# A four-layer graph network on one core: pair records on 16-byte places, edge weights from 64-row products, and a reordered second addition

## Chip, cores, metric

The kernel runs on one core of a Trainium2 chip. The metric is the device time of one execution in microseconds, median of the runs. Engines: PE is TensorE's matmul and PEld its weight load, DVE is VectorE, ACT is ScalarE, POOL is GpSimd, SP is SyncE. A name with a q (DVEq) is the engine's sequencer: waits, register steps, register loads and the issue of transfers.

## Reference

A graph of 3125 nodes (160 features: 64 scalars and 32 vectors of 3) and 100,000 edges passes through four message-passing layers. Each layer normalizes the nodes, maps them linearly to a table, gathers a table row for every edge, multiplies it (in layers 0, 1 and 3) by weights that a small network of the edge's attributes gives, adds the result over the edges of each target node, multiplies the sums by weights and updates the nodes. Layer 0, cut to its core:

```
w = relu(edge_feature @ W_fc1) @ W_fc2                  # 64 -> 64 -> 224 per edge
xs, xv = s[dst], v[dst]
out0a = w0 * xs                                         # and four more products of w with xs, xv and the edge's direction
agg = segment_sum(concatenate([out0a, ...]), src, N) / 32
node += gate(agg @ W_out + skip)
```

Layer 1 has 10 attributes and 100 hidden units, layer 3 has 8 and 64; layer 2 has no such network: it adds the gathered rows, scaled by the edge's 4 direction values.

## The kernel before, in words

**Tiles.** Edges are sorted by target. A tile is 128 edges (one per partition) whose targets lie in one bin of 32 nodes. There are 880 tiles, in 110 groups (GROUPS) of GT = 8; a group is PAIRS = 4 pairs. The first part of the program ranks the edges by bins, scatters and copies the edge rows into tile order in DRAM (POOL's scatters L752, SP's and ACT's copies L522 to L526) and makes small tables: for each tile its bin, its first node, its column and the half group in which that column has arrived (tiles, L1300 to L1343; written to DRAM by SP from L625, and read back after layer 0 into `guide`, one record of RECORD = 18 words per group: 8 bins, 8 places in the ring, 2 counts).

**Edge stage.** Per layer (LAYERS, n = 0 to 3) an edge stage of 110 groups runs on all engines, each with its own loop over pairs of groups (pipeline), tied by semaphores:
- SP loads the group's edge rows (edge_rows, L609).
- POOL gathers table rows for 128 edges with one indirect transfer: in layer 0 once per tile (L881, 880 of them), in layers 1 to 3 once per column of 128 sorted edges (L920, 782 of them) into a ring of 16 columns. It waits for landings three gathers behind (landed_column, L896) and, per half ring, until the columns' tiles have been used (`free`, loaded by L906, 4 words).
- PE transposes the edge rows (turn, L1854/L1857), forms the hidden units of the next group at u = 2 (hidden, L1864 for layer 0, L1867 for 1, L1871 for 3), per pair the edge weights (weights, L1891) and, two pairs later, the sums over edges (sums, L1915 and L1917; L1911 in layer 2). PE is in order: at step u it does weights(i), sums(i - 2), then turn or hidden.
- ACT turns the hidden units into SBUF (L1067) and builds the selection matrices, 24 or 32 activations a group (L1084).
- DVE, for each pair i, first adds the sums of pair i - 3 to the accumulators (flush, L1495, two additions, where each waits until the one before has ended, since both may hit one bin), then multiplies weights and gathered rows (products, L1509 and L1512 for one tile in layers 1 and 3, L1525 and L1529 in layer 0). At u = 2 it makes the one-hot matrix of the next group (select, L1476, L1486). At the head of each group it loads registers: 8 bins in layer 0 (L1538), the 18-word record in layers 1 and 3, its first 8 words in layer 2 (L1542); in layer 2 PE loads 10 words of it (L1924).

A helper (L99) computes values to wait for from loop registers. The weights of both tiles of a pair go into one PSUM bank (4 or 5), 224 columns apart. The weight matrices of layers 0 and 3 stand twice, in rows 0 to 63 and 64 to 127 with zeros in the other half, and the product runs over all 128 rows; in layers 1 and 3 the hidden products do the same with four or two copies. A float32 product is two records of PE and two of PEld in the trace.

Between edge stages the sums are turned and multiplied by the layer's weights and the nodes updated (node steps).

## Time and profile before

| | us |
|---|---|
| median of 3 runs (lowest, highest) | 8134.93 (8115.99, 8168.47) |
| span of the profiled execution | 5998.2 |
| PE busy in the span | 4489.1 |
| POOL busy | 4014.9 |
| DVE busy | 3441.9 |
| ACT busy | 3414.1 |

The profile gives the profiled execution's span, from its first to its last instruction. Of that execution no other time is given; the median of the runs is 2136.7 us longer, and that part lies outside of what the profile shows. In timeline rows the columns are start, duration, engine, line, operation, names, shapes, count and in brackets the idle time before; in a row of one line they are the count, the durations in ns (lowest/median/highest) and the first and last start in us.

### The profile page before, as it was taken

The page shows a single profiled execution, that of the slowest core. Times are in us where ns is not written, and L with a number is a line of the kernel's source. Part 1 is how long each engine was busy: PE and PEld are TensorE (multiplying, and loading weights), DVE is VectorE, ACT ScalarE, POOL GpSimd, SP SyncE. Part 2 cuts the span into 40 slices and gives each one's busy share as a digit, 9 for nine tenths or more (in the row PEclk, how much of TensorE's full clock was granted, in tenths as well). Part 3 has the DMA queues.
Part 4 walks back from the last instruction along what each step waited for, and adds up shares of the span by engine and source line. Part 5 has one row for each costly group of instructions (what it writes and reads, how often), then busy time and mean ns, then how long its engine had stood idle before and what let it go on. Part 6 is the DMA issues. An engine that isn't in the chain of part 4 may idle for free.

```text
span 5998.2 us, 122036 instructions
## 1 busy us (share of the span) xinstructions
PE 4489.1 (75%) x24426; PEld 3923.9 (65%) x24427; DVE 3441.9 (57%) x11481; ACT 3414.1 (57%) x14717; POOL 4014.9 (67%) x4467
## 2 busy tenths in 40 slices
PE   7793121599999998788888886555555888888888
PEld 5552110588888888788888885444444877777777
DVE  8894000577777776566666664333333666666666
ACT  0000000366555554677777776677778677777775
POOL 6777777677777764676666646777777376666654
PEclk8896555799999999899999996555555899999999
DMA  8533333344444441222222212333333122222221
GB/s 307 181 80 74 80 79 82 77 88 88 87 88 88 88 87 36 71 73 70 68 68 65 64 48 69 77 78 77 78 79 79 44 74 70 68 67 64 64 62 41
DMA packets 643946, 484.25 MB, mean 81 GB/s; under 512 B 437482, under 2 KB 551593, under 8 KB 643707
## 3 DMA queue, kind: packets, MB, share of 16 engines
q0 software_dynamic: 181776, 292.84, 19.4%
q1 hardware_dynamic: 379563, 149.21, 10.3%
q10 hardware_dynamic: 82496, 40.92, 2.3%
q8 instruction: 45, 0.74, 0.1%
q14 instruction: 66, 0.54, 0.0%
HBM read 400.40 MB, written 96.88 MB: 83 GB/s over the span
## 4 chain that ended last, share of the span: by engine, by line
issue 28%; PE 22%; DVE 11%; DMA 9%; DVEq 6%; POOL 4%; ACT 1%; POOLq 1%; SPq 0%; ACTq 0%
DMA gath<-table,rows 6%; DVE acc L1495 5%; PE bank L1915 4%; PE bank L1891 4%; PE bank L1917 4%; PE bank L1867 3%; DVEq L1542 3%; PE bank L1911 2%; DMA gath<-table,small 2%; PE bank L1971 2%; DVE work L1512 2%; DVE work L1509 2%; POOL gath L920 2%; POOL gath L881 2%; DVE work L1529 1%
## 5 line engine op out<-in xcount | busy, mean ns | idle before, releaser
L920 POOL DMA_INDIRECT gath<-table,small x2346 | 2226.1, 949 | 1069.8 <-issue 611.7
L1084 ACT ACTIVATE sel<-acc,rows 128x32 f32<-128x32 f32 x10560 | 2292.6, 310 | 302.3 <-DVE acc L1486 247.6
L1495 DVE TENSOR_TENSOR acc<-acc,bank 128x160 f32 (+1 forms) x3520 | 1207.4, 343 | 1476.3 <-issue 583.1
L1915 PE MATMUL bank<-work,sel 128*128 128x160 f32 (+1 forms) x5280 | 1353.2, 339 | 342.4 <-DVE acc L1495 342.0
L1915 PEld LDWEIGHTS bank<-work,sel 128*128 128x128 f32 x5280 | 914.5, 196 | 420.0 <-DVE acc L1495 396.4
L1917 PE MATMUL bank<-work,sel 128*128 128x160 f32 x5280 | 1181.1, 306 | 0.0
L1891 PE MATMUL bank<-w,work 128*128 128x224 f32 (+2 forms) x5280 | 1153.8, 342 | 17.6 <-DVE work L1529 8.9
L881 POOL DMA_INDIRECT gath<-table,rows x880 | 832.0, 945 | 348.2 <-issue 196.2
L1891 PEld LDWEIGHTS bank<-w,work 128*128 128x128 f32 (+1 forms) x5280 | 915.7, 195 | 89.7 <-issue 52.1
L1917 PEld LDWEIGHTS bank<-work,sel 128*128 128x128 f32 x5280 | 937.8, 196 | 44.7
L752 POOL DMA_INDIRECT rows_a<-acc x782 | 754.6, 965 | 280.3 <-issue 237.5
L1911 PE MATMUL bank<-gath,sel 128*128 x1760 | 554.5, 491 | 450.6 <-POOLq L896 277.3
L1911 PEld LDWEIGHTS bank<-gath,sel 128*128 128x128 f32 x1760 | 454.3, 325 | 550.8 <-issue 550.8
L1067 ACT ACTIVATE work<-bank 100x512 f32<-100x512 f32 (+1 forms) x440 | 250.6, 596 | 786.3 <-PE bank L1871 283.8
L1084 ACT ACTIVATE sel<-sel,rows 128x32 f32<-128x32 f32 x2640 | 582.2, 308 | 124.6 <-DVE sel L1486 97.1
L1512 DVE TENSOR_TENSOR work<-bank,gath 128x192 f32<-128x192 f32 x1760 | 610.9, 347 | 0.0
L1509 DVE TENSOR_TENSOR work<-bank,gath 128x128 f32<-128x128 f32 x1760 | 499.8, 284 | 76.2 <-PE bank L1891 33.0
L1529 DVE TENSOR_TENSOR work<-bank,gath 128x288 f32<-128x288 f32 x880 | 357.1, 447 | 0.0
L997 ACT ACTIVATE acc<-acc 128x69 f32 (+1 forms) x34 | 9.2, 272 | 599.7 <-DMA acc<-in_rows_a 516.3
L1788 PE MATMUL bank<-acc,ident 100*128 100x391 f32 (+3 forms) x1000 | 347.7, 439 | 0.0
L1525 DVE TENSOR_TENSOR work<-bank,gath 128x256 f32<-128x256 f32 x440 | 185.2, 421 | 244.8 <-POOLq L869 244.7
L1716 PE MATMUL bank<-ident,sel 128*64 128x128 f32 x25 | 10.2, 407 | 396.3 <-ACT sel L980 396.3
(296 smaller groups left out, 3998.6 us busy)
## 6 DMA issues: line engine op xcount, KB each, us to landing
rows<-rows_b SPq DMA_DIRECT2D x330, 128.0 KB
gath<-table,small POOLq DMA_INDIRECT x2346
rows_a<-acc ACTq DMA_DIRECT2D x1, 30360.0 KB, 102.9
rows<-rows_a SPq DMA_DIRECT2D x110, 256.0 KB
acc<-in_rows_a SPq DMA_DIRECT2D x34, 793.5 KB
gath<-table,rows POOLq DMA_INDIRECT x880, 2.6
acc<-in_rows_b SPq DMA_DIRECT2D x34, 368.0 KB, 3.7
rows_a<-acc POOLq DMA_INDIRECT x782
```

Source lines behind the costliest of these rows:

```text
L752: pool.indirect_dma_start(rows_dram[0][:, :], bass.IndirectOffsetOnAxis(ap=pos_r[q][:, u:u + 1], axis=0), stage[0][q][:, u * A_W:(u + 1) * ...
L881: pool.indirect_dma_start(gath[q][:, u, :], None, table_dram[n][:, :], bass.IndirectOffsetOnAxis(ap=flat[:, u * w + first:u * w + first + ...
L920: pool.indirect_dma_start(gath_all[:, u, :], None, table_dram[n][:, :], bass.IndirectOffsetOnAxis(ap=index_r[q][:, u:u + 1], axis=0)).then ...
L1084: i = act.activation(sel[q][:, t, at:at + BIN], hot, ACT.Copy, scale=e[:, k:k + 1])
L1495: dve.tensor_tensor(sums, sums, bank(6 + b, P, 256 * h, 256 * h + L.width), ALU.add).then_inc(S["fl"].sem, 1)
L1509: dve.tensor_tensor(ps, wt[:, 0:128].rearrange("p (w c) -> p w c", w=2), one[:, 0:S0].unsqueeze(1).to_broadcast([P, 2, S0]), ALU.mult)
L1512: ins = dve.tensor_tensor(pv, wt[:, 128:L.wcols].rearrange("p (w m) -> p w m", w=nv) .unsqueeze(2).to_broadcast([P, nv, 3, V1]), one[:, S0 ...
L1529: ins = dve.tensor_tensor(pv, wt[:, h, 128:L.wcols].rearrange("p (w m) -> p w m", w=nv) .unsqueeze(2).to_broadcast([P, nv, 3, V1]), two[:, ...
L1891: ins = pe.matmul(bank(4 + u % 2, P, 224 * h, 224 * h + L.wcols), hid, w, start=True, stop=True, skip_group_check=True)
L1911: ins = pe.matmul(out, sel[qv][:, t, 0:128], gath_flat[:, bass.ds(slots[t], NF)] if L.compact else gath[qv][:, t, :], start=True, stop=Tru ...
L1915: pe.matmul(out, sel[qv][:, t, 96:224], work[:, a + NF:a + NF + L.width], start=True, stop=False, skip_group_check=True)
L1917: ins = pe.matmul(bank(6 + b, P, 256 * h, 256 * h + NF), sel[qv][:, t, 0:128], work[:, a:a + NF], start=False, stop=True, skip_group_check ...
```

## The change

1. A record is 4 words per pair of tiles (two bins, two columns), written so by SP into DRAM in three transfers and read back in one; it starts at a multiple of 16 bytes. DVE loads it at each pair of layers 1 to 3, PE at each pair of layer 2. The place in the ring is computed from the column (column & 15, times 160) in the engine's registers. `arrived` counts columns, not half groups, and is waited for at each pair.
2. The weights of layers 0 and 3 are products over the 64 rows that hold the tile's values, the two tiles of a pair in different halves of the rows and in different banks (4 and 5, or 2 and 3). The hidden products of layer 1 run over 32 rows each into four banks, those of layer 3 over 64 rows each into two; ACT reads them with one activation.
3. DVE makes the first addition of a pair ahead of the products, as before, and the second between the products of the two tiles (in layer 0 between the scalar product of both and the vector products).

```diff
-RECORD = 2 * GT + 2
+RECORD = 4
+RECORDS = (GROUPS + 1) * PAIRS
+TILE_MASK, COLUMN_MASK = 1023, 1023
...
+        def weight_banks(n, u):
+            if n in (0, 3):
+                return (4, 5) if u % 2 == 0 else (2, 3)
+            return 4 + u % 2, 4 + u % 2
+        def weight_place(n, u, h):
+            return weight_banks(n, u)[h], 224 * h if n == 1 else 0
...
+        def pair_record(kind, i):
+            _, record = nc.values_load_multi_w_load_instructions(
+                guide[0:1, bass.ds(i * RECORD, RECORD)], engines=(kind,), min_val=0, max_val=COLS - 1, ...)
+            bins = [nc.s_assert_within(v, 0, BINS - 1, ...) for v in record[0:2]]
+            return bins + list(record[2:4])
+        def ring_column(column):
+            return gath_flat[:, bass.ds((column & (RING_COLS - 1)) * NF, NF)]
...
-            sp.dma_start(guide_dram[:, :], rows_i[2:5, :]).then_inc(s_written, 16)
+                sp.dma_start(records[:, 0:LAG_FL, 0:2], pairs_of[2:3, 0:LAG_FL, :]).then_inc(s_written, 16)
+                sp.dma_start(records[:, LAG_FL:, 0:2], pairs_of[2:3, 0:RECORDS - LAG_FL, :]).then_inc(s_written, 16)
+                sp.dma_start(records[:, :, 2:4], pairs_of[3:4, 0:RECORDS, :]).then_inc(s_written, 16)
...
+            sp.dma_start(guide, guide_dram[:, :]).then_inc(s_nodes_of, 16)
...
-                    last = is_static(r) and r * RING_COLS + u == COLS - 1
-                    pool.sem_inc(S["arrived"].sem if u % HALF == HALF - 1 or last else s_apart["pool"], 1)
+                    pool.sem_inc(S["arrived"].sem, 1)
...
-                            wait(pool, S["sc"] if n == 2 else S["prod"], free[h])
+                            wait(pool, S["sc"] if n == 2 else S["prod"], free[h] & TILE_MASK)
...
-                def flush(i, u, bins, n=n, L=L, S=S):
+                def flush(i, u, h, bins, n=n, L=L, S=S):
                     b = (u - L.lag_fl) % 2
-                    wait(dve, S["sc"], i * 2 - (2 * L.lag_fl - 2))
-                    for h in range(2):
...
+                    if h == 0:
+                        wait(dve, S["sc"], i * 2 - (2 * L.lag_fl - 2))
+                    wait(dve, S["fl"], i * 2 - (2 * L.lag_fl - h))
...
-                        if 2 * u % HALF == 0:
-                            wait(dve, S["arrived"], need[2 * u // HALF])
-                            dve.sem_inc(s_apart["dve"], 1)
+                        wait(dve, S["arrived"], (record[3] & COLUMN_MASK) + 1)
+                        dve.sem_inc(s_apart["dve"], 1)
...
+                            one, at = ring_column(record[2 + h]), (2 * u + h) * L.row
...
+                            if h == 1:
+                                between()
...
-                            i = pe.matmul(bank(2, P, 256 * k, 256 * k + 256), w1[3][:, k, :], attrT[:, 0:256],
-                                          start=True, stop=True)
+                            rows_of = slice(64 * k, 64 * k + 64)
+                            i = pe.matmul(bank(k, P, 256, 512), w1[3][rows_of, k, :], attrT[rows_of, 0:256],
+                                          start=True, stop=True, skip_group_check=True)
...
-                        return hid[:, 128 * (t // 2):128 * (t // 2) + 128], w2[0][:, t % 2, :]
+                        return hid[half, 128 * (t // 2):128 * (t // 2) + 128], w2[0][half, t % 2, :]
...
-                        ins = pe.matmul(bank(4 + u % 2, P, 224 * h, 224 * h + L.wcols), hid, w,
+                        at_bank, first = weight_place(n, u, h)
+                        ins = pe.matmul(bank(at_bank, P, first, first + L.wcols), hid, w,
...
-                        if L.compact and n == 2:
-                            wait(pe, S["arrived"], need[v // 2])
-                            pe.sem_inc(s_apart["pe"], 1)
+                    if n == 2:
+                        wait(pe, S["arrived"], (columns[1] & COLUMN_MASK) + 1)
+                        pe.sem_inc(s_apart["pe"], 1)
```

## Rows read from the trace of the kernel before

**Rows 1.** Profile page, part 4, the chain of waits by engine.
```profile
issue 28%; PE 22%; DVE 11%; DMA 9%; DVEq 6%; POOL 4%; ACT 1%; POOLq 1%; SPq 0%; ACTq 0%
```

**Rows 2.** L1495, VectorE's additions, in the edge stages of layers 0 to 3.
```profile
L1495 DVE TENSOR_TENSOR acc<-acc,bank x880: 405/420/423, 1119.7 to 2288.8; 128x256 f32 x176
...
L1495 DVE TENSOR_TENSOR acc<-acc,bank x880: 306/320/323, 2430.6 to 3582.1; 128x160 f32 x176
...
L1495 DVE TENSOR_TENSOR acc<-acc,bank x880: 320/321/323, 3658.8 to 4657.8; 128x160 f32 x176
...
L1495 DVE TENSOR_TENSOR acc<-acc,bank x880: 306/320/323, 4756.1 to 5937.7; 128x160 f32 x176
```

**Rows 3.** L920, gathers of layer 2; POOL's timeline in layer 1.
```profile
L920 POOL DMA_INDIRECT gath<-table,small x782: 940/946/1197, 3643.3 to 4648.7; - x196
...
3001.08 0.95 POOL L920 DMA_INDIRECT gath<-table,small  x1 [0.30 <-issue]
```

**Rows 4.** Windows, layers 0, 1, 3: PE, PEld, DVE, ACT, POOL busy; granted clock.
```profile
1200.00:2200.00 1000.00, 955.98 (x5054) 845.58 (x5053) 731.46 (x1966) 596.54 (x2430) 707.87 (x750) 1.00 0.42 88
2500.00:3500.00 1000.00, 885.59 (x5539) 821.86 (x5538) 639.69 (x2483) 775.36 (x3346) 654.79 (x723) 0.99 0.27 68
4850.00:5850.00 1000.00, 823.45 (x5022) 781.99 (x5022) 625.82 (x2418) 715.27 (x3153) 635.72 (x703) 0.95 0.26 66
```

**Rows 5.** Chain of waits in layer 1: start, us, what.
```profile
3001.24 3.57 issue
...
3005.48 0.06 DVEq L1495
3005.58 0.33 DVE acc L1495
...
3009.05 1.73 PE bank L1867 x8
3010.78 0.65 PE bank L1891 x4
```

**Rows 6.** TENSOR_LOAD: layer 0, two neighbouring groups of layer 1, POOL.
```profile
L1538 DVEq TENSOR_LOAD <-tile_bins_row x111: 594/598/854, 1112.1 to 2284.1; - x111
...
L1542 DVEq TENSOR_LOAD <-acc x1: 4055/4055/4055, 3000.7 to 3000.7; - x1
...
L1542 DVEq TENSOR_LOAD <-acc x1: 1570/1570/1570, 3012.6 to 3012.6; - x1
...
L906 POOLq TENSOR_LOAD <-tile_bins_row x144: 315/324/348, 2435.4 to 5888.5; - x144
```

**Rows 7.** L99, register steps of a helper, on VectorE's sequencer.
```profile
L99 DVEq ALU_OP  x5646: 40/40/47, 658.5 to 5930.0; - x195
...
L99 DVEq FUSED_REGOPS  x2650: 46/53/57, 1132.3 to 5911.3; - x190
```

**Rows 8.** VectorE's timeline in layer 1: two additions and the next product.
```profile
3006.84 0.77 DVE L1495 TENSOR_TENSOR acc<-acc,bank 128x160 f32 x2
3007.53 0.28 DVE L1509 TENSOR_TENSOR work<-bank,gath 128x128 f32<-128x128 f32 x1
```

**Rows 9.** Timeline of PE, PEld: layer 0's preparation, transposes after layer 0.
```profile
805.62 0.69 PE L1726 MATMUL bank<-wps,sel 64*128 64x64 f32 x2
...
806.23 0.50 PEld L1727 LDWEIGHTS bank<-wpv,sel 96*128 96x128 f32 x2
...
807.57 0.74 PE L1729 MATMUL bank<-wpv,sel 96*128 96x96 f32 x2
...
807.89 0.23 PEld L1716 LDWEIGHTS bank<-ident,sel 128*64 128x64 f32 x1
...
2336.94 1.04 PE L1963 MATMUL bank<-ident,acc 128*128 128x128 f32 x8
```

**Rows 10.** SP's transfers after the tile tables: start, us.
```profile
305.72 0.48 SPq L628 DMA_DIRECT2D release<-acc  x1
316.73 0.39 SPq L543 DMA_DIRECT2D acc<-in_rows_a  x1
```

More of the change, by code:

```diff
@@ L527, in copy_tiles @@
                                   given_dram[bass.ds(start[w], P), :].unsqueeze(1)).then_inc(s_copy[part], 16)
+        def pair_record(kind, i):
+            _, record = nc.values_load_multi_w_load_instructions(
+                guide[0:1, bass.ds(i * RECORD, RECORD)], engines=(kind,), min_val=0, max_val=COLS - 1,
+                skip_runtime_bounds_check_because="bins and columns of tiles")
+            bins = [nc.s_assert_within(v, 0, BINS - 1, skip_runtime_bounds_check_because="bins") for v in record[0:2]]
+            return bins + list(record[2:4])
+        def ring_column(column):
+            return gath_flat[:, bass.ds((column & (RING_COLS - 1)) * NF, NF)]
         block = ctx.enter_context(nc.Block())
@@ L1498, in products @@
-                def products(i, g, u, half, q, slots, need, n=n, L=L, S=S):
+                    if h == 0:
+                        wait(dve, S["sc"], i * 2 - (2 * L.lag_fl - 2))
+                    wait(dve, S["fl"], i * 2 - (2 * L.lag_fl - h))
+                    sums = acc[:, bass.ds(bins[h] * L.width, L.width)]
+                    dve.tensor_tensor(sums, sums, bank(6 + b, P, 256 * h, 256 * h + L.width),
+                                      ALU.add).then_inc(S["fl"].sem, 1)
+                def products(i, g, u, half, q, record, between, n=n, L=L, S=S):
@@ L1540, in edges, with flush_second @@
                             skip_runtime_bounds_check_because="counts of at most BINS bins, less one")
-                    else:
-                        _, record = nc.values_load_multi_w_load_instructions(
-                            guide[0:1, bass.ds(g * RECORD, RECORD if L.mlp and L.compact else GT)], engines=(DVE,), min_val=0,
-                            max_val=(RING_COLS - 1) * NF, skip_runtime_bounds_check_because="bins, places in the ring, counts of half groups")
-                        bins = [nc.s_assert_within(v, 0, BINS - 1, skip_runtime_bounds_check_because="bins") for v in record[0:GT]]
-                        slots, need = record[GT:2 * GT], record[2 * GT:]
-                    for u in range(PAIRS):
-                        i = g * PAIRS + u
+                    for u in range(PAIRS):
+                        i, record = g * PAIRS + u, None
+                        if n:
+                            record = pair_record(DVE, i)
+                        pair_bins = record[0:2] if n else bins[2 * u:2 * u + 2]
+                        def flush_second(i=i, u=u, pair_bins=pair_bins):
+                            if within(i - L.lag_fl, TILES // 2):
+                                flush(i, u, 1, pair_bins)
                         if within(i - L.lag_fl, TILES // 2):
-                            flush(i, u, bins)
+                            flush(i, u, 0, pair_bins)
                         if L.mlp and within(i, TILES // 2):
-                            products(i, g, u, half, q, slots, need)
+                            products(i, g, u, half, q, record, flush_second)
+                        else:
+                            flush_second()
                         if u == 2 and within(g + 1, GROUPS):
@@ L1761, in rows_of_tiles @@
                 pe.wait_ge(s_tiletab, o + 1)
-                count = 5 if o else 1
+                count = 4 if o else 1
                 for c in range(TCOLS):
@@ L1884, in hidden_of, with weights @@
                     a = (k // 2 * 2 + quad) * 128
-                    return hid[:, a:a + 128], w2[3][:, k % 2, :]
-                def weights(i, u, q, L=L, S=S, hidden_of=hidden_of):
+                    return hid[half, a:a + 128], w2[3][half, k % 2, :]
+                def weights(i, u, q, n=n, L=L, S=S, hidden_of=hidden_of):
                     wait(pe, S["prod"], i - 1)
@@ L1921, in edges @@
                 def edges(g, half, q, n=n, L=L, S=S, turn=turn, hidden=hidden, weights=weights, sums=sums):
-                    slots = need = None
-                    if L.compact and n == 2:
-                        _, record = nc.values_load_multi_w_load_instructions(
-                            guide[0:1, bass.ds(g * RECORD + GT, GT + 2)], engines=(TENSOR,), min_val=0, max_val=(RING_COLS - 1) * NF,
-                            skip_runtime_bounds_check_because="places in the ring, counts of half groups")
-                        slots, need = record[0:GT], record[GT:]
                     for u in range(PAIRS):
@@ L1934, in edges @@
                         if within(i - L.lag_sc, TILES // 2):
-                            sums(i, g, u, half, q, slots, need)
+                            sums(i, g, u, half, q)
                         if L.mlp and within(g + 1, GROUPS):
```

96 lines of the change are left out of this document (44 added, 52 removed).

## Prediction

> **What bounds the kernel now.** I read the chain of waits first. "issue" leads it with 28%, PE follows with 22%, POOL has 4% [rows 1]: time goes where an engine waits for nothing that the profile names. The kernel is four edge stages in a row, each of 110 groups of 8 tiles, so next I took their lengths from the first and the last addition (L1495) of each [rows 2]: 1169.1 us for layer 0, 1151.5 for layer 1, 998.9 for layer 2, 1181.6 for layer 3. By group that is 10.63, 10.47, 9.08 and 10.74 us. The same kind of stage runs at 9.08 where there are no products, so that is the first thing to explain.
>
> Layer 2 is bound by the gathers. 782 of them start between 3643.3 and 4648.7, one in 1.287 us; a single one is 0.95 busy and 0.30 of issue, back to back [rows 3]. 782 gathers for 110 groups make 7.11 in a group, so this floor is 9.15 us per group for each of layers 1 to 3. Layer 0 gathers by tile: 8 x 1.25 = 10.0 us, and the rest up to 10.63 is some longer landings. PE is busy 956 us of 1000 there [rows 4], close to POOL's limit; POOL's 880 issues do not wait for it, since PE comes behind them.
>
> Layers 1 and 3 stand 1.3 and 1.6 us over the floor. The chain in layer 1 shows why [rows 5]: 3.57 us of "issue" in front of VectorE's first addition of a group, then PE in an unbroken row. This is VectorE's register load: 4055 ns for the 18 words of one group, 1570 ns for the next group [rows 6]. The pattern is the record's place: 18 words are 72 bytes, so every second record starts off a multiple of 16 bytes. A load costs 595 ns for 8 words in layer 0 and 324 ns for POOL's 4 words (both start on multiples of 16 bytes), so about 75 to 80 ns a word against 4055/18 = 225 ns. Two groups spend 4.06 + 1.57 = 5.6 us in loads, hidden only for the first 0.3 or so. Besides, VectorE is busy 639.7 us in 95.5 groups, 6.7 a group [rows 4], with four waits of 0.13 between additions and the selection's own, together some 7.5: 2 x 7.5 + 5.6 = 20.6 for two groups that take 2 x 10.47 = 20.9. PE is nearly as full: 885.6 us of the same 1000, 9.27 us a group [rows 4].
>
> **The change part by part.**
> *Records.* VectorE loads 4 words per pair of tiles, each record on a multiple of 16 bytes. Bounds: 4 x 75 = 300 ns (595/2) and 4 x 225 = 900 ns if the alignment wanted is 32 bytes. POOL's row has 4-word loads at both 16-byte places and a spread of only 315 to 348 ns [rows 6], so I take 0.32.
> Against this stands the Trainium skill, "Runtime: NRT & Kernel Launch", Instruction fetch mechanics: a register load is about 200 ns for each register, however many are loaded. The 4055 ns record agrees with it (225 ns a word), POOL's 324 ns for 4 words and the 595 ns for 8 do not [rows 6]; by it the four loads would be 3.2 us a group, which is rival B.
> Four loads of 0.32 are 1.28 us a group against (4.06 + 1.57)/2 = 2.81. More goes through the sequencer, though: now a pair takes some 11 register steps (6 of its own instructions and (5646 + 2650)/1760 = 4.7 of L99 [rows 7]) at 0.10 us from one to the next (3005.48 to 3005.58 [rows 5]), 1.15 us in all. The change adds the load, its address (0.10), a count and wait for every pair (0.20) and a mask and a product in four ring addresses (0.12 in all; nothing shows that form, bounds 0 and 0.4): 1.87 us a pair. With the selection of the next group (0.85) and half a loop's turn (0.25) it is 8.6 us a group. The additions and products themselves need less, so the sequencer, not the arithmetic, is VectorE's limit afterwards.
>
> *Second addition moved.* Two additions of 0.32 us [rows 2] take 0.77 with the idle time between them, so the second starts 0.45 after the first: it waits until that has ended. The next product starts 3007.53 - 3006.84 = 0.69 after the first, 0.24 after the second [rows 8], and 0.24 is what an addition costs where nothing is waited for. So about 0.2 us a pair comes off VectorE's path, 0.8 a group. It is in the 8.6, since the sequencer stands still in that wait today. In return the bank of that second sum comes free about 0.7 us later in the pair; PE's sums four pairs behind want it, and one pair is over 2 us, so it costs nothing while VectorE is not late. In layer 0 VectorE has 1000 - 731 us to spare [rows 4]; nothing comes of it there.
>
> *Weights over 64 rows, hidden products over 32 or 64.* Two products of one pair go to different rows of the array and to different banks. If they run side by side a pair of weights falls from 0.65 us (192 columns [rows 5]; 0.76 for 224) to half at best, to nothing gained at worst. The loads of the stationary operand sit between: the trace never shows them closer than about 0.11 us (eight transposes with their loads in 1.04, in which the last one's length is contained [rows 9]), and I take that: a pair's four loads are 0.43, so 0.33 a pair is gained in layer 0, 0.22 in layer 3. Layer 1's hidden products are 1.73 us a group [rows 5]; 8 loads by the same value leave 0.86, all four side by side 0.43. Layer 3's fall by 0.4.
> Against it stands the change of mode. In the preparation of layer 0, products over 64 and 96 rows alternate: the weight load of L1727 starts at 806.23, just 0.08 before L1726's last product ends at 806.31. Between L1729 (96 rows) and L1716 (128 rows) it starts at 807.89, 0.43 before L1729 ends at 808.32 [rows 9]. So only the step between 64 rows and more keeps the next load from running ahead. With the step a product takes 0.61 to 0.67 us from start to start ((807.57 - 806.23)/2) against two loads of 2 x 0.11 at a granted clock of 0.5, 0.43 together: up to 0.24 lost; I take 0.18 at full clock, between 0.12 (all of it scales) and 0.24 (none). Layer 0 and layer 3 have 8 such steps a group, 1.44 us, layer 1 has 2.
> The Trainium skill says the same and more in "TensorEngine Tiling (Array Packing)", Key Properties: changing the tiling mode drains the engine, while tiles inside one mode run in parallel. The trace agrees with the first half, by 0.08 against 0.43 us [rows 9]; no row here shows the second.
> PE by group: layer 0 10.2 (956 us in 94.1 groups) - 1.3 + 1.4 = 10.3; layer 1 9.27 - 0.87 + 0.36 = 8.75; layer 3 8.85 (823.5 in 93 groups) - 0.9 - 0.4 + 1.4 - 0.3 (the granted clock of 0.95 should rise, since the 3 us stalls go) = 8.65.
>
> *Waits by column.* VectorE and PE wait for their own pair's column, not for the half group's. It lets them follow POOL more closely. POOL itself gets one mask per half ring beside a gather's 0.95 us: nothing, at most 4 x 0.04 in 16 gathers, 6 us a layer.
>
> *Small parts.* SP writes three small transfers of records instead of one, at 305; it then stands idle from 306.2 to 316.7 [rows 10], and the few us that 882 short pieces take to issue fit in that. Five linked operations on VectorE in the prologue go, 1 us, beside POOL's scatter. Layer 1's six loads of records become one, while SP waits for a memset behind it anyway. ScalarE's hidden activation is one of 1024 columns instead of two: the same work; ScalarE is at 775/95.5 = 8.1 us a group [rows 4].
>
> **Sum.** What is late next in layers 1 and 3 is POOL: 9.15 against 8.6 (VectorE), 8.65 to 8.75 (PE) and about 8.4 (ScalarE). Four engines within 8% of each other do not run at the floor; I add 0.2 in layer 1 and 0.35 in layer 3. Layer 1: 110 x (10.47 - 9.35) = 123 us off. Layer 3: 110 x (10.74 - 9.5) = 136 off. Layer 0: PE is as near as before and starts more slowly after each wait, +10. Layer 2: 0, bounds -10 and +6. Together -249 us, the span 5998 to 5749. Median of the runs and span differ by 2136.7 us; the profile shows nothing of what lies outside its span and the change does nothing there that I can name, so it is carried over: 8134.9 - 249 = 7886 us, 3.1% less.
>
> **The rivals.**
> *A. The sequencer takes the place of the load.* If the masks and ring addresses cost 0.1 us each, a pair is 2.15 and a group 9.7, near 10.0 with waits: layer 1 gives 52, layer 3 75 to 80 us: about 8010. For it: VectorE would then be behind POOL. Against: 0.1 is a step by itself, and these can be folded in.
> *B. The short loads stay slow.* At 225 ns a word it is 0.9 us a load, 3.6 a group instead of 2.8, less the 0.8 of the moved addition: no change, 8130. POOL's loads speak against it.
> *C. Slower: the change of mode costs more than I read.* The place is layer 0, where PE has 0.5 us to spare. With a price c per step its PE is 8.9 + 8c a group, over 10.63 from c = 0.22 on; layer 3's is 7.25 + 8c, over 10.74 from 0.44. With c = 0.4 layer 0 loses 160, layer 1 gives 115 and layer 3 32: 8148. From there on the total is slower; with c = 0.5 layer 0 loses 250 and layer 3 56, layer 1 gives 105: 8336. For it: drain and load are bare in rows 9. Against: they were 0.24 there at half the clock.
> *D. All at the floor:* layers 1 and 3 at 9.1: 151 + 180 us off, 7800.
>
> **Chances.** Forecast 0.60, D 0.10, A 0.14, B 0.05, C 0.08, something unseen of either sign 0.03. Range: from the floor's 7780 to 8050 (A with some of C); what is left out is B, C and little more. 1% is 81 us and is about what a measurement of this kernel can tell. Faster by over 1%: the forecast, D and most of A, 0.81; within 1%: B, the rest of A and the mild half of C, 0.12; slower 0.07.
>
> **What would show it.** Right: VectorE's loads at about 0.32 us, four a group, and no 3.57 us "issue" in the chain of layers 1 and 3; two thirds of POOL's gathers there 1.25 us apart; layer 2's length unchanged; additions between products with no idle time before the second; granted clock 1.0 in layer 3. Weights (L1891) of a pair starting together. Wrong: loads of 0.9 (B); VectorE without idle time while POOL waits for L1512 (A); PE idle or late at each step between weights and sums and layer 0 over 1200 us (C).

## The result, and the profile after

| | us |
|---|---|
| before, median of 4 runs (lowest, highest) | 8127.75 (8115.99, 8168.47) |
| after, median of 4 runs (lowest, highest) | 8313.6 (8310.11, 8321.43) |
| ratio after to before, 95% interval | 1.0224 [1.0198, 1.025] |
| span of the profiled execution of after | 8308.6 |

The change makes the kernel 2.2% slower, where 3.1% faster was forecast. The last row of the table already says what went wrong. The profiled execution of after took 8310.11 us, 1.5 us more than its span (1.4 to 2.8 us in all executions on record). So almost nothing lies outside a span, and the 2136.7 us that the forecast put there did not exist: the profile of before (span 5998.2) is of an execution that took about 6000 us, and the timed ones took 8128. The same kernel runs in two settings. In one batch of the experiments the kernel before had a median of 5995.48 us (5991.46 to 6005.3), in the four others 8113 to 8141. The batches ran on four chips, the first on one and the others on three more. With only one batch near 6000 us, the chip and the batch can't be told apart. I call them the short and the long setting. The profile of before comes from the short one, the two medians and the profile of after from the long one.

So rows of after can't be held against rows of before as they stand. The nearest to before in the long setting is w1 below (before with three masks and products over fewer rows, 8143.33 us). First VectorE's additions in the profile of after, layers 0 to 3 (count, durations in ns, first and last start in us); they answer [rows 2].

```profile
L1512 DVE TENSOR_TENSOR acc<-acc,bank x880: 406/413/423, 1708.5 to 3402.2; 128x256 f32 x176
...
L1512 DVE TENSOR_TENSOR acc<-acc,bank x880: 309/320/323, 3541.4 to 5159.6; 128x160 f32 x176
...
L1512 DVE TENSOR_TENSOR acc<-acc,bank x880: 320/321/323, 5244.8 to 6543.3; 128x160 f32 x176
...
L1512 DVE TENSOR_TENSOR acc<-acc,bank x880: 309/320/323, 6644.0 to 8248.0; 128x160 f32 x176
```

The same rows of w1:

```profile
L1507 DVE TENSOR_TENSOR acc<-acc,bank x880: 407/421/423, 1709.7 to 3380.0; 128x256 f32 x176
...
L1507 DVE TENSOR_TENSOR acc<-acc,bank x880: 307/320/323, 3521.2 to 5141.6; 128x160 f32 x176
...
L1507 DVE TENSOR_TENSOR acc<-acc,bank x880: 314/320/323, 5218.3 to 6427.4; 128x160 f32 x176
...
L1507 DVE TENSOR_TENSOR acc<-acc,bank x880: 307/320/323, 6526.2 to 8103.9; 128x160 f32 x176
```

Read them in two steps. An addition lasts 320 ns in both settings, as in [rows 2]: VectorE's arithmetic is not slower. But w1's stages are 1670, 1620, 1209 and 1578 us long against 1169, 1152, 999 and 1182 in [rows 2], and the first addition comes at 1709.7, not 1119.7. The time that was taken to lie outside the span is in every stage, and ahead of the first. It is not in the node steps between the stages: from one stage's last addition to the next one's first it is 141.2, 76.7 and 98.9 us in w1 and 141.1, 76.7 and 97.8 in b1, the same kernel in the short setting but for the products' rows. Second, from w1 to after: layer 0 +23, layer 1 -2, layer 2 +89, layer 3 +26 us. Layer 2, where the forecast expected nothing, holds most of the loss.

What differs inside a stage is seen in the sequencers. Register steps of after, whole run, by engine (answering [rows 7]), and its loads (answering [rows 6]):

```profile
L102 DVEq ALU_OP  x7186: 2/40/1394, 1081.6 to 8243.1; - x200
L102 PEldq FUSED_REGOPS  x2650: 3/42/1392, 1732.6 to 8219.6; - x190
L102 DVEq FUSED_REGOPS  x2650: 1/53/1277, 1736.6 to 8224.0; - x190
L102 PEldq ALU_OP  x1768: 3/36/1287, 1082.1 to 8219.1; - x197
...
L543 DVEq TENSOR_LOAD <-acc x1326: 3/343/1392, 3525.4 to 8246.9; - x190
...
L543 PEldq TENSOR_LOAD <-acc x440: 4/332/1394, 5226.4 to 6540.9; - x147
```

The medians are those of [rows 7], 40 and 53 ns. The third number is new: up to 1394 ns, where [rows 7] had 47 and 57. Counting single records in the traces, steps of 0.6 to 0.8 us (four in five within 10 ns of 0.70) occur 1 time in the profile of before, 1226 times in w1 and 2286 times in after. In layer 2 they are 391 in w1 and 963 in the changed kernel (a2 below), of which PE has 10 and 459. They fall on any step of a loop, a register operation or a semaphore increment alike: 459 of 4287 steps of PE in layer 2, 11%. The first number is new as well: steps of 1 to 3 ns and a load of 3 ns, where the fastest step was 40 ns in [rows 7] and the fastest such load is 339 in a1 below. A load can hardly be done in 3 ns, so what moved there may be the time written into the record and not the step.

Two other differences can be weighed against this. The granted clock is lower, 0.81 to 0.85 in layers 0, 1 and 3 of w1 against 0.95 to 1.00 in b1, and PE's products last longer for it. But in layer 2 it is 0.51 against 0.52, and w1's layer 2 is 208 us longer all the same. The transfers are not slower: a packet of the gathers' queue takes 102 ns on average in w1 and in b1.

Three more signs of the long setting. The longest waits of after (waited for: us in total, times, longest):

```profile
ACT work L1090 <- remote: 1267.6, 172, 13.0
POOL gath L938 <- DVE work L1531: 1243.7, 219, 10.5
PEld bank L1943 <- DVE acc L1512: 991.4, 547, 9.9
PEld bank L1939 <- issue: 875.9, 518, 14.0
PE bank L1943 <- DVE acc L1512: 833.3, 302, 11.0
```

Single waits last 10 us and more, and "remote" names no maker although ScalarE waits there for PE. The semaphore updates in the trace explain it: of the updates of PE's sums (a2) 900 of 3086 come over 0.3 us after the end that the trace gives for the product, p99 7.1 us; of VectorE's additions 1 of 2722, and in the short setting (a1) 1 of 3470 and 1 of 3446. PE's ends are modelled, so PE may itself have been late. With so many updates late or absent, who released whom is uncertain in all readings of waits in this setting. Second, the chain of waits, which answers [rows 1]:

```profile
PE 2%; issue 1%; DVEq 1%; DVE 1%; another core or an unknown queue 1%; ACT 0%; POOL 0%; ACTq 0%; POOLq 0%
```

It covers 6% of the span instead of most of it: the trace of the long setting lacks over half of its semaphore updates (45,775, against 111,892 in the profile of before), and the chain can't be followed back. Third, the windows of after (layers 0 to 3; columns as in [rows 4]):

```profile
1850.00:3350.00 1500.00, 1137.58 (x5231) 808.18 (x5232) 753.67 (x2040) 610.77 (x2528) 731.17 (x773) 0.85 0.29 61
3600.00:5100.00 1500.00, 1038.05 (x5889) 915.64 (x5890) 698.18 (x2645) 833.19 (x3456) 693.09 (x766) 0.83 0.19 48
5300.00:6500.00 1200.00, 577.23 (x1606) 399.17 (x1607) 315.04 (x1002) 728.37 (x3204) 684.17 (x756) 0.53 0.24 60
6700.00:8200.00 1500.00, 1004.07 (x5526) 786.99 (x5527) 700.98 (x2663) 795.06 (x3478) 697.16 (x770) 0.80 0.19 49
```

POOL issues 773 gathers in 1500 us of layer 0, against 750 in 1000 us before. No engine is near full: PE, 956 of 1000 in [rows 4], has 1138 of 1500. This is a kernel that waits at its handovers, and nothing of PE's or VectorE's limits, on which the forecast rests, holds in it.

One count fits the lengths of the stages. Call every instruction in the trace, steps of the sequencers included, and every semaphore update a record, the updates counted in the short setting's trace, which has them. In b1 the four stages take 24.4, 24.2, 28.5 and 24.5 ns a record. In w1 (updates of b1) they take 34.8, 33.2, 34.4 and 32.7, in a2 (updates of a1) 35.2, 31.9, 34.1 and 32.0. The node steps between the stages take 34.8 to 36.4 ns a record in b1 already, and they are the one part that w1 does not lengthen. So it looks as if the long setting lets through one record in 32 to 35 ns, whatever the engine. This is my estimate from counts. No run tests it, and in particular none tells whether the limit is on the work or on the recording of it. Each timed execution has a span and a granted clock on record, so none is known to have run unrecorded.

### The profile page after: what moved, and what is told of

Its sections match the earlier page's. It is cut to its first block and busy times, and to the rows that moved or that the text cites. A ratio compares the mean times of both kernels' runs of the same rounds, so it can differ in the third digit from the quotient of the medians.

```text
span 8308.6 us, 130589 instructions
## 1 busy us (share of the span) xinstructions
PE 4994.0 (60%) x24426; PEld 3801.1 (46%) x24427; DVE 3467.1 (42%) x11476; ACT 3461.2 (42%) x14607; POOL 4008.5 (48%) x4467
## 5 line engine op out<-in xcount | busy, mean ns | idle before, releaser
L1943 PE MATMUL bank<-work,sel 128*128 128x160 f32 (+1 forms) x5280 | 1641.8, 398 | 1009.5 <-DVE acc L1512 833.3
L1943 PEld LDWEIGHTS bank<-work,sel 128*128 128x128 f32 x5280 | 999.6, 223 | 1338.1 <-DVE acc L1512 991.4
L1945 PE MATMUL bank<-work,sel 128*128 128x160 f32 x5280 | 1336.6, 340 | 0.0
L1917 PE MATMUL bank<-w,work 64*128 64x224 f32 (+2 forms) x5280 | 1044.4, 409 | 450.6 <-ACT work L1090 329.2
L1945 PEld LDWEIGHTS bank<-work,sel 128*128 128x128 f32 x5280 | 1086.7, 225 | 67.9
L1939 PE MATMUL bank<-gath,sel 128*128 x1760 | 630.2, 503 | 682.9 <-issue 399.9
L1917 PEld LDWEIGHTS bank<-w,work 64*128 64x128 f32 (+1 forms) x5280 | 643.2, 213 | 751.3 <-issue 674.2
L1090 ACT ACTIVATE work<-bank 128x512 f32<-128x512 f32 (+1 forms) x330 | 243.8, 739 | 1679.7 <-remote 1267.6
L1080 ACT ACTIVATE attrT<-bank 128x256 f32<-128x256 f32 (+1 forms) x330 | 149.0, 452 | 813.3 <-remote 298.6
L1385 DVE COPY_PREDICATED acc<-work,bank 128x391 f32<-128x391 int16 (+3 forms) x500 | 253.2, 506 | 507.0 <-remote 325.8
L1810 PE MATMUL bank<-work,acc 128*128 128x391 bf16 (+3 forms) x500 | 163.3, 327 | 430.4 <-issue 344.8
```

The costliest lines, as they stand in the source:

```text
L1917: ins = pe.matmul(bank(at_bank, P, first, first + L.wcols), hid, w, start=True, stop=True, skip_group_check=True)
L1939: ins = pe.matmul(out, sel[qv][:, t, 0:128], ring_column(columns[h]), start=True, stop=True, skip_group_check=True)
L1943: pe.matmul(out, sel[qv][:, t, 96:224], work[:, a + NF:a + NF + L.width], start=True, stop=False, skip_group_check=True)
L1945: ins = pe.matmul(bank(6 + b, P, 256 * h, 256 * h + NF), sel[qv][:, t, 0:128], work[:, a:a + NF], start=False, stop=True, skip_group_check ...
```

## Experiments

Five batches; in each the kernel before was timed beside the others, which tells the setting. Kernels built on before carry masks on three loaded counts (`need[...] & 1023` twice, `free[h] & 1023`). Layer lengths are from the first to the last start of an addition in the profiled execution.

### Short setting (before 5995.48 us)

**b1, before with the masks.**


> The kernel before with three masks on loaded counts, otherwise unchanged. Theory S (the sequencers are slower in the timed executions than in the profile of before that was read): this profile's span is near 8130, not 5998, its register steps on VectorE take well over the 40 and 58 ns mean of the profile of before, and 600 ns of extra time show up in single steps. Theory O (2137 us lie outside the span): span near 6000 and time near 8130. Time against before: within 0.5% either way.


Measured: 6037.03 us, ratio 1.0069 [1.0052, 1.0085]; layers 1171, 1183, 1001, 1183. Span and time differ by 2.3 us, so theory O fails; S can't be judged here, since the time itself is 6037 in this batch. Three masks that nobody would have priced cost 42 us, 31 of them in layer 1. They stand in front of waits of VectorE and POOL, and of PE in layer 2. This is the base for s1.

**r1, records per pair alone.**
```diff
-                        if L.mlp and within(i, TILES // 2):
-                            products(i, g, u, half, q, record, flush_second)
-                        else:
-                            flush_second()
+                        flush_second()
+                        if L.mlp and within(i, TILES // 2):
+                            products(i, g, u, half, q, record, lambda: None)
```
and the weights and hidden products as before.


> Only the records per pair, the ring addresses and the waits by column; weights over 128 rows in one bank, both additions ahead of the products. Theory S: the added register steps (some 5 a pair on VectorE, some 5 on PE in layer 2) cost more than the shorter loads save, so most of the loss of 186 us stands here, 1.5 to 3% slower than before. Rival W (the change of mode on PE costs the time): this kernel is 1 to 3% faster than before, as was forecast for records.


Measured: 5924.21 us, 0.9883 [0.9866, 0.9899]; layers 1168, 1131, 996, 1134. The records gain here, by the 1 to 3% of rival W and against theory S, which was meant for the other setting.

**s1, the moved addition alone** (before with masks, second addition between the products).


> The kernel before (with the masks) with VectorE's second addition between the products. Both theories: little, 0 to 1% faster, as it only takes an idle 0.2 us a pair off VectorE and adds no instruction. If it is slower by over 0.5%, a later free sum bank holds up PE's sums.


Measured: 6069.49 us, 1.0126 [1.0109, 1.0143]; layers 1172, 1276, 997, 1125. Neither theory had a loss: 32 us more than b1. With the slow 18-word loads still there, layer 1 loses 93 us to b1 and layer 3 gains 57. Why the two differ I did not test.

**a1, records and moved addition**, products over 128 rows as before:
```diff
-                if n in (0, 3):
-                    return (4, 5) if u % 2 == 0 else (2, 3)
...
-                    hid, half = hid_t(n, q), slice(64 * (t % 2), 64 * (t % 2) + 64)
+                    hid, half = hid_t(n, q), slice(0, 128)
```
and the hidden products in one bank or two.


> The changed kernel with the weights and hidden products back over 128 rows and in one bank; records and second addition as changed. Rival W: 2% or more faster than the changed kernel, near or under before. Theory S: as slow as the changed kernel within 1%, or slower, since PE's products side by side save something.


Measured: 5749.35 us, 0.9592 [0.9576, 0.9608]. The rows of its additions, layers 0 to 3:

```profile
L1506 DVE TENSOR_TENSOR acc<-acc,bank x880: 405/411/423, 1119.8 to 2284.8; 128x256 f32 x176
...
L1506 DVE TENSOR_TENSOR acc<-acc,bank x880: 308/320/324, 2424.0 to 3468.9; 128x160 f32 x176
...
L1506 DVE TENSOR_TENSOR acc<-acc,bank x880: 320/321/323, 3545.7 to 4543.8; 128x160 f32 x176
...
L1506 DVE TENSOR_TENSOR acc<-acc,bank x880: 308/320/323, 4640.1 to 5686.1; 128x160 f32 x176
```

Layers 1 and 3 take 1045 and 1046 us where 1028 and 1045 were forecast. The load and the register steps of layer 1 and the largest waits there:

```profile
L541 DVEq TENSOR_LOAD <-acc x443: 339/344/628, 2408.2 to 3467.7; - x148
...
L541 DVEq FUSED_REGOPS  x424: 53/75/93, 2436.0 to 3447.5; - x142
```
```profile
POOL gath L936 <- issue: 214.5, 658, 2.6
ACT work L1083 <- PE bank L1883: 158.5, 110, 3.8
DVE acc L1506 <- issue: 109.1, 373, 0.8
```

A load is 0.344 us, no "issue" before an addition is over 0.8 us (3.57 in [rows 5]) and no wait there for PE over 1.1, and 658 of 782 gathers follow the one before with nothing but issue between.

### Long setting

**a2, the changed kernel again** (before 8113.38 us in this batch).


> The changed kernel as it is. If it runs where the kernel before takes about 5995 us: theory E (the slow timed runs are a property of where they ran, in which every register step is dearer) says 5700 to 5800, 3 to 5% faster than before, and register steps at 40 to 60 ns again. Theory S (the change itself makes the sequencers stall) says above before with the long register steps seen in the changed kernel's first profile. Within E, if the change of mode costs PE what was read, layer 0 is 1165 to 1185 us and layers 1 and 3 are 1030 to 1050.


Measured: 8317.48 us, 1.0244 [1.0207, 1.028]; layers 1674, 1627, 1307, 1614. k1 and m1 repeat it in two other batches, in the hope of the short setting, which did not come: 8304.45 us, 1.0228 [1.0193, 1.0262], and 8317.6 us, 1.0218 [1.0188, 1.0249]; g3 in a third, 8308.79 us, 1.0206 [1.018, 1.0232].

**a3, the changed kernel with both additions ahead of the products** (the diff of r1).


> The changed kernel with both additions ahead of the products again. Records alone gave 5924, records with the moved addition 5749 where before took 5995, so by the theory that the moved addition is worth about 0.2 us a pair on VectorE once its loads are short, this is 130 to 180 us slower than the changed kernel, in layers 1 and 3. Rival: with PE's products side by side PE is no longer last and the additions' place is worth under 50 us.


Measured: 8258.12 us, 1.0164 [1.0125, 1.0203]; layers 1661, 1599, 1311, 1607. The moved addition, worth 175 us in the short setting (5924 to 5749), costs 59 here.

**w1, only the products over fewer rows** (before with masks, and the change's banks, 64 and 32 rows).


> The kernel before (with masks, 6037) with the weights over 64 rows and the hidden products over 32 or 64, nothing else. Theory: VectorE's loads of 4.06 and 1.57 us stay, so layers 1 and 3 stay at 1150 to 1185 and the total is within 0.7% of before with masks. If PE sets the pace of layer 1 too, its 0.87 us a group less give up to 95 us. If the change of mode costs more than 0.22 us a step, layer 0 is over 1180.


Measured: 8143.33 us, 1.0036 [1.0013, 1.0059], masks included.

**h1, the changed kernel with edge weights over 128 rows**, hidden products as changed.


> The changed kernel with the edge weights of layers 0 and 3 back over 128 rows, the hidden products as changed. Against the changed kernel it has 8 changes of mode a group fewer in layer 0 and some 6 fewer in layer 3. If these steps cost more than the pair side by side saves (0.33 and 0.22 us a pair), layers 0 and 3 are faster here by up to 50 us together; if not, the same or slower by as much. Layer 1 is the same in both.


Measured: 8305.04 us, 1.0218 [1.018, 1.0255], 12 us under a2: nothing that can be told apart. Its batch gave PE's rows for the two forms, though. Layer 0 of a2 (start, us, what):

```profile
1855.37 0.59 PE L1943 MATMUL bank<-work,sel 128*128 128x256 f32 x2
1855.80 0.43 PE L1945 MATMUL bank<-work,sel 128*128 128x160 f32 x2
1856.17 0.65 PE L1917 MATMUL bank<-w,work 64*128 64x224 f32 x4
```

From the weights' start to the next sums' start the median of a pair is 0.759 us in h1 (0.757 in a1; 436 pairs each) and 0.579 in a2 (437). The two tiles of a pair start 7 ns apart, so they do run side by side. Each of the two changes of mode costs, at a granted clock of 1.0. The step from 128-row sums to 64-row weights is 0.229 us from the last sum's start, where 128-row weights follow after 0.136: 0.093 us. On the way back the first step inside the sums is 0.320 us against 0.216: 0.104 us. From one pair's weights to the next pair's, with only the sums between, it is 2.184 us in a2 and 2.166 in h1, and the group that waits least is 10.03 us in a2 and 9.95 in h1. So in layer 0 the two changes eat up what the products side by side save.

**g4, records per pair alone, here** (the kernel of r1; before 8140.67 us).


> Records per pair alone (products over 128 rows, both additions ahead of the products). Where before takes 8113 us: theory S: slower than before by 100 to 160 us, nearly all of the change's loss, with layer 2 at about 1305 us against 1209. Rival (the loss comes from the parts on PE and from the moved addition): within 50 us of before. Where before takes 5995 us it should repeat 5924 within 15 us.


Measured: 8242.24 us, 1.0117 [1.0093, 1.0142]; layers 1678, 1608, 1303, 1601. 102 of the 168 us that the changed kernel loses in this batch, and nearly all of layer 2's part (94 of 99 us over w1), come with the records.

**g2, more register steps and no load.** In layer 2 PE makes three waits more per pair, all long satisfied:
```diff
+                    if n == 2:
+                        for k in range(1, 4):
+                            wait(pe, S["fl"], i * 2 - (2 * L.lag_sc + 2 * RING - 2) - 2 * k)
+                            pe.sem_inc(s_apart["pe"], 1)
```


> The kernel before with three masks on loaded counts, and in layer 2 PE makes three further waits per pair of tiles that are always satisfied already, each with its own register step and an increment of a spare semaphore: some 2,600 sequencer records more, no load, no wait that could hold. Theory S: where the kernel before takes 8113 us, layer 2 grows by 60 to 120 us (from 1209 us), as it did under the change, which adds 2,179 PE records there; where before takes 5995 us it grows by under 10. Rival (loads or the column waits make layer 2 longer): no growth over 20 us in either place.


Measured: 8279.75 us, 1.0183 [1.0153, 1.0213]. Layer 2's additions:

```profile
L1495 DVE TENSOR_TENSOR acc<-acc,bank x880: 320/321/324, 5226.8 to 6563.4; 128x160 f32 x176
```

1337 us against 1209 in w1, for 2583 more PE records (counted in the traces, 5128 against 2545): 50 ns each, though none waits for anything. Steps alone make the layer longer, without loads and without waits by column. They stand on PE's own path: its steps, loads and increments in the layer take 636 us here and 307 in w1, so this run needs no limit that engines share.

**k2, the same number of steps on SyncE, which has little to do** (before 8114.23 us):
```diff
+                    if n == 2:
+                        for k in range(1, 13):
+                            wait(sp, S["sel"], g * 2 - 2 - 2 * k)
+                            sp.sem_inc(s_apart["sp"], 1)
```


> The kernel before with three masks on loaded counts, and in layer 2 SyncE makes twelve further waits per group that are always satisfied already, each with its register step and an increment of a spare semaphore: some 2,600 records more on an engine that has little to do. Where before takes about 8120 us: if the records of all engines share one limited resource, layer 2 grows by 60 us or more from 1209 us (PE's 2,583 further records made it 1337); if each engine pays for its own records only, it stays within 15 us. Where before takes about 5995 us nothing changes over 10 us.


Measured: 8212.62 us, 1.0112 [1.0079, 1.0146]. Layer 2, and SyncE's steps in it:

```profile
L1499 DVE TENSOR_TENSOR acc<-acc,bank x880: 307/320/323, 5227.0 to 6492.3; 128x160 f32 x176
```
```profile
L99 SPq ALU_OP  x1296: 1/33/1397, 5231.6 to 6473.0; - x186
```

1265 us, 56 more than w1, a little under the 60 that I had set; far over the 15 of the rival. It looks like a shared limit, but the run doesn't show one, because SyncE was not out of the way. The steps stand in front of its issue of the edge rows, and the 0.7 us steps on it rise from 94 to 487. In one group SyncE starts on them at 5484.65 us and issues the rows only at 5499.41, where a group lasts 11.6 us. VectorE's wait for these rows, in layer 2:

```profile
DVE small L1480 <- DMA rows<-rows_b: 282.5, 57, 12.6
```

In w1 VectorE is idle at that place for 2.9 us in all, and never for this transfer. From issue to use the rows have 5.1 us in w1 and 2.2 in k2 (medians). So each engine paying for its own steps can explain k2 as well, and whether steps on an engine that nobody waits for cost anything stays open. The 0.7 us steps of the others did not grow: VectorE has 119 against 204 in w1, PE 1 against 10.

**g1, the changed kernel with one 16-word load per group.**
```diff
+            _, words = nc.values_load_multi_w_load_instructions(
+                guide[0:1, bass.ds(g * (PAIRS * RECORD), pairs * RECORD)], engines=(kind,), ...)
```


> The changed kernel, but VectorE (and PE in layer 2) loads the four 4-word records of a group in one load of 16 words at the head of the group, on a multiple of 16 bytes. Everything else of the change stays. At about 75 ns a word the load is 1.2 us, against four of 0.34. Theory S (each step and load of a sequencer is dear where the kernel before takes 8113 us): some 13 records a group of VectorE and of PE go, so it is 30 to 80 us faster than the unchanged new kernel there, most of it in layer 2. Where before takes 5995 us, steps cost nothing much, and one long load at the head of the group is bare: 0 to 60 us slower than the new kernel. Rival W (the wait for each pair's column is what costs in layer 2): within 20 us of the new kernel in both places, since the waits stay.


Measured: 8249.17 us, 1.0138 [1.0115, 1.0161]; layer 2 1267 us, 41 less than the changed kernel, for 1293 records less. k3 is the same kernel in another batch: 8240.27 us, 1.0136 [1.0102, 1.017].

**m2, lean:** the load of g1, columns waited for once per half group, both additions ahead of the products, 128 rows (before 8137.47 us in the batch of m2 and m3).
```diff
-                        wait(dve, S["arrived"], (record[3] & COLUMN_MASK) + 1)
+                        if u % 2 == 0:
+                            wait(dve, S["arrived"], (of_pairs[u + 1][3] & COLUMN_MASK) + 1)
```


> The changed kernel's aligned records, but loaded once per group in 16 words, columns waited for once per half group, both additions ahead of the products, all products over 128 rows. Theory (time goes with sequencer records where before takes about 8120 us): layer 2 at 1215 to 1245 us, the whole at 8120 to 8180 us, so within 1% of before. Rival (something else in the records costs): 8220 or more, as records per pair alone (8242). Where before takes about 5995 us: 5900 to 5950, as records per pair alone (5924).


Measured: 8108.53 us, median of 10 runs, 0.9963 [0.9944, 0.9982]: faster than both kernels in the long setting, by 0.4% and 2.5%, and just under what I had set. Layers 1661, 1594, 1204, 1529. Layers 2 and 1:

```profile
L1510 DVE TENSOR_TENSOR acc<-acc,bank x880: 314/321/323, 5191.9 to 6395.8; 128x160 f32 x176
...
L1510 DVE TENSOR_TENSOR acc<-acc,bank x880: 307/321/323, 3511.7 to 5105.7; 128x160 f32 x176
```

**m3, lean with the second addition between the products.**


> The same with the second addition between the products. Where before takes about 8120 us: 40 to 70 us slower than m2_lean, if the moved addition costs by itself, as it did with records per pair (8317 against 8258); within 20 us of it, if it costs only through the number of records. Where before takes about 5995 us: 5740 to 5800, some 150 faster than m2_lean.


Measured: 8217.86 us, 1.0099 [1.0065, 1.0133]. The moved addition costs 109 us, with the same records, more than the 40 to 70 expected. PE's waits in layer 1, first m2, then m3:

```profile
PE bank L1913 <- ACT work L1087: 250.0, 57, 8.0
PE bank L1939 <- DVE acc L1510: 55.2, 47, 4.7
```
```profile
PE bank L1940 <- DVE acc L1510: 193.6, 78, 7.8
PE bank L1914 <- ACT work L1087: 177.4, 38, 11.7
```

By these rows PE's wait for the bank that an addition sets free grows from 55 to 194 us, while its wait for ScalarE falls from 250 to 177. In this setting the releasers are uncertain, so the 109 us are measured and their way through PE is likely, not shown.

## Why the prediction was wrong

**The step that failed** is the last of its sum: "Median of the runs and span differ by 2136.7 us; the profile shows nothing of what lies outside its span and the change does nothing there that I can name, so it is carried over". The difference was not outside. An execution ends 1.5 us after its span, and w1's span is longer than b1's by 2130 us: 590 ahead of the first addition, then 499, 438, 208 and 395 in the four stages, and under 2 between and behind them. The 2136.7 us were the sign that the profile was of another setting than the times, and every duration and every floor came from it. A span a quarter shorter than the median should have made all its terms suspect, and I gave that no rival and no chance. With it fell the terms added to it. The forecast had +10, -123, 0 and -136 us for layers 0 to 3; from w1 to a2, in the setting of the times, they are +4, +7, +98 and +37.

**In the setting that it was read from, the terms hold**, as far as they were run (a1, without the products over fewer rows):
- Records and loads: 0.344 us a load against 0.32, and the bare 3.57 us gone. Rival B (225 ns a word) is refuted. The Trainium skill's 200 ns per register ("Runtime: NRT & Kernel Launch", Instruction fetch mechanics) does not fit these loads either: 4 words in 0.344 us is 86 ns a word. The page speaks of registers loaded from HBM at the start of a program; these come from a tile in SBUF. That the place matters, and not the number of words alone, the trace of before shows in layer 2: the same 8 words of a record take 0.60 us in one group and 1.86 in the next (medians), as the record's start is on a multiple of 16 bytes or 8 bytes off it.
- The sequencer as VectorE's limit (8.6 a group) stayed under POOL's floor; rival A did not come in the short setting.
- The moved addition: 0.8 us a group forecast; from r1 to a1 layer 1 falls by 86 us and layer 3 by 88, 0.79 and 0.80. But only with short loads: with the old ones s1 loses 32 us, and the forecast, which added the two terms, could not see that.
- Layer 0 (+10 forecast) and 2 (0) were 1165 and 998 us against 1169 and 999.
- Span 5749 forecast, 5746.8 measured in a1. That the two agree so closely is partly luck: the forecast had the products over fewer rows in it and a1 has not.

**Products over 64 rows:** both sizes were forecast at nearly twice what was measured. A pair saves 0.18 us in layer 0 (0.33 forecast), and the two changes of mode cost 0.093 and 0.104 (0.18 each). The two errors cancel: layer 0's PE is 10.03 us a group against 9.95, 0.08 longer, where 0.1 was forecast. That is luck. In layer 1 the hidden products go from 1.73 to 0.62 us (a2), where 0.86 was forecast. Rival C, slower from a price of 0.22 on, is refuted by the price. That the two tiles run side by side, which no row of before showed, is now shown, as "TensorEngine Tiling (Array Packing)", Key Properties, in the Trainium skill has it. In the long setting PE has idle time everywhere and the parts give nothing that can be measured (h1 12 us under a2). What they give in the short one is open, since the changed kernel as a whole never ran there.

**In the long setting** other things count. From w1 to a2 layer 2 grows by 98 us, for 2179 PE and 647 VectorE records more: 35 ns a record, where g2 has 50 and g1 gives back 32. In layers 1 and 3 VectorE has some 2300 records more each, and what they cost and what the shorter loads give cancel: -12 and +23 us in g4 against w1. "It is in the 8.6, since the sequencer stands still in that wait today" was true of VectorE and blind to the others. On the bank of the second sum the forecast wrote that "it costs nothing while VectorE is not late"; in the long setting the reordering costs 59 (a3) to 109 us (m3), as if VectorE were late there. So the loss (168 to 204 us by batch) is about 100 for records and 60 for the moved addition; what remains, up to 40, I can't assign, but w1, with its masks, is 30 us over before.

**Open:** what makes the long setting. The runs show steps of 0.70 us on all sequencers and PE's semaphore updates late (1% of a2's by over 7.1 us). They do not show that one engine's steps hold up another's: g2 and k2 have their steps on a path that the stage waits for. The steps of 0.70 us can't be all of it either. Layer 0 of w1 has 138 of them on all engines, 97 us together, and is 499 us longer. The best fit is one record in 32 to 35 ns, as estimated above, and the first rival is then the recording of the trace itself. The count is no exact law: m2's layer 2 has 858 instruction records more than w1's and is 5 us shorter, 33.4 ns a record against 34.4. The price of the masks alone was not taken in the long setting.

## What to carry to other kernels

Hold the profiled execution's own time against the timed runs before anything is read from it; where they differ by more than per cents, ask which durations differ (the longest of a group of register steps beside its median tells) rather than carrying the difference over. Load register records in few, larger loads on multiples of 16 bytes, and, where the longest steps of a profile are far over their median, count the sequencer's steps, waits and increments as a cost of their own: of the versions with the new records, the one with fewest of them was the only one that did not lose there. Whether that cost is there without the recording is not known. Before an engine is called idle, look for who waits for the transfers that it issues. A reordering that takes a wait off one engine and hands a buffer on later is worth its sum only while the other engine is not waiting for that buffer.

## What was not expected of the hardware

- The same program takes 5995 us in one batch and 8113 to 8141 in others, with additions of 320 ns in both, equal node steps between the stages, and sequencer steps of 0.70 and up to 1.4 us among those of 40 ns. Over half of the semaphore updates are absent from the trace of the long setting.
- The stages of the long setting take 32 to 35 ns for each instruction and semaphore update, those of the short one 24 to 29 (b1); an estimate from counts.
- Twelve waits a group that are met already, on SyncE, can last 15 us in the long setting and make VectorE wait for SyncE's transfers (57 times, 282.5 us).
- A 4-word register load on a multiple of 16 bytes takes 0.344 us (median of a1's layer 1, lowest 0.339), and 16 words 1.10 us (m2's layer 1); 18 words took 4.06 us off such a place [rows 6], and 8 words 1.86 us against 0.60 on it (layer 2 of before).
- Two products of a pair in different halves of the rows and different banks start 7 ns apart; the step from 128 to 64 rows costs 0.093 us and the one back 0.104, so in layer 0 nothing is gained.
- Three masks on loaded values cost 42 us of 5995 in the short setting.
